# Cross-attention with image tokens: the values of the image tokens in four column tiles of TensorE, those of the last text tokens in two

## The chip, the core and the metric

The kernel runs on one core of a Trainium2 chip. The time is the device time of one execution in microseconds (us). TensorE (PE) multiplies and transposes into PSUM, VectorE (DVE), ScalarE (ACT) and GpSimd (POOL) work element by element, and all DMAs here are issued by SyncE (SP), whose queue is in order. Every engine runs its own instructions in order and waits for the others on semaphores.

## What is computed

Two batches of 2048 queries (640 wide) attend to 154 context tokens (1024 wide) in 20 heads of 32. The first 146 tokens are text; the last 8 are image tokens (4 dummies and 4 that carry a box mask), with key and value weights of their own and a softmax of their own. The two results are added, projected, and the input is added.

```python
text, ip_h = ctx[:, :146], ctx[:, 146:]
q = heads(x @ w_q)
out = merge(sdpa(q, heads(text @ w_k), heads(text @ w_v)))
out += merge(sdpa(q, heads(ip_h @ w_k_ip), heads(ip_h @ w_v_ip), mask=box_mask))
y = out @ w_out + b_out + x
```

## The kernel before

The queries are cut into 16 blocks of 256. A first iteration, the setup, makes the keys and values of both batches while it makes the queries and the maxima of scores of block 0. The 16 iterations behind it each finish one block and prepare the next. The instructions of every engine stand in an order written out by hand (`STEPS`), which all engines walk through; semaphores tie them together.

The change lies in the setup. The 154 tokens of a batch are split as 128 text tokens ("batch 0", "batch 1"), the last 18 text tokens ("rest", both batches together: 36 rows) and 8 image tokens ("ip", both batches: 16 rows). Their values are a product over 1024 = 8 chunks of 128 (`CC`), in plain fp32, 640 columns wide. `V_UNITS` (L93) lists eight units, two for each kind of token (512 and 128 columns); `V_PLACES` (L94) says ahead of which step a pair of units is made: ip ahead of the transposes X 0, rest ahead of the scores S(1,0), batch 0 ahead of S(2,0), batch 1 at the end of the setup. All of them are written by the matmul of L835, `make_values`.

What follows a unit:

- ACT copies it out of PSUM (L496 for ip and rest, L499 for batch 0 and 1) and counts `s_vc`.
- For batch 0 and 1, DVE splits the value in three bf16 parts: subtract from PSUM (L653, `v_left`), cast (L656, SBUF to SBUF), subtract again (L658, two inputs in SBUF). These stand in DVE's order ahead of the reductions of S(2,0) (L706, L707), which free the score banks for S(2,1) on PE.
- For ip and rest, SP moves 16 small pieces into `v_tail` (L362, L365), once `s_vc` says that both are copied.
- After batch 0, ACT converts the output weights (L528, `wo_hi`), and POOL makes their remainder (L438, `wo_lo`, one instruction on 128x3200).

Around this stand, in the setup: SP's 12 DMAs that build the key stack of batch 1 (L347, `k_stack`); POOL's two memsets of `k_tail` (L435), which wait for those DMAs to land, and stand ahead of `wo_lo` in POOL's order; on DVE the split of the maxima (L716 cast, L718), eight copies into `k_tail` (L666), and the split of batch 1. PE leaves the setup when the split of the last unit has read PSUM (`s_vsplit` at 10), among other waits, and begins iteration 1 with the transposes of L923.

Of the kernel before, what the change touches and what calls it, by code (L numbers as in the profile page):

```python
# [89 lines left out]

V_UNITS = [(keys, c0, c1) for keys in ("ip", "rest", "batch 0", "batch 1") for c0, c1 in ((0, 512), (512, D))]  # L93
V_PLACES = {("X", 0): (0, 1), ("S", 1, 0): (2, 3), ("S", 2, 0): (4, 5), None: (6, 7)}  # L94
W_O_PLACE = ("S", 2, 0)
COUNTS = {0: (0, 3), 1: (3, 4), 3: (4, 7), 4: (7, 8)}

# [66 lines left out]
def attention_kernel(nc, x, ctx, boxes, wq, wk, wv, wk_ip, wv_ip, wo, b_out,  # L164
# [5 lines left out]
    with ExitStack() as stack:  # L170
        def sb(name, shape, dt=F32, where=stack):
            return where.enter_context(nc.sbuf_tensor(name, shape, dt))
# [25 lines left out]
        with ExitStack() as setup:  # L198

            ctx_main = sb("ctx_main", [P, BATCHES, CTX_D], where=setup)  # L200
            ctx_rest = sb("ctx_rest", [P, CTX_D], where=setup)
            mask = sb("mask", [IP, SEQ], where=setup)

            w_k_ip = sb("w_k_ip", [P, CC, D], where=setup)

            w_kv = sb("w_kv", [P, CC, D], where=setup)
            ctx_t = sb("ctx_t", [P, CC, BATCHES * CTX], where=setup)
            rest_t = sb("rest_t", [P, CC, BATCHES * TAIL], where=setup)
            small = sb("small", [16, 256], where=setup)
            pick = sb("pick", [16, BATCHES * IP], BF16, setup)  # L210
            with ExitStack() as first:
                row_raw = sb("row_raw", [STACK - ROW_MASK, 4 * CTX], where=first)
                row_consts = sb("row_consts", [STACK - ROW_MASK, 4 * CTX], F32R, first)
            v_rest = sb("v_rest", [BATCHES * REM, D], where=setup)
            v_rest_ip = sb("v_rest_ip", [BATCHES * IP, D], where=setup)
            v_left = sb("v_left", [P, 512], where=setup)

        w_v_ip = wo_raw[:, 0:CC, :]
# [77 lines left out]
        def v_bank(n):  # L296

            return bank[4 + n % 4]
# [7 lines left out]
        def _(sp):  # L306
# [43 lines left out]
            def rest_of_setup():  # L350


                sp.wait_ge(s_vp, 2)
                sp.dma_start(wo_raw[:, KC:2 * KC, :], wo.rearrange("(c p) n -> p c n", p=P)).then_inc(s_wo, 16)
                keys_to_stack(1)

                sp.wait_ge(s_ones, 16 * BATCHES)
                sp.wait_ge(s_vc, 4)
                for b in range(BATCHES):
                    for j in range(4):  # L360
                        r = 32 * j
                        sp.dma_start(v_tail[b][r:r + REM, :, VW * j:VW * j + DH],  # L362
                                     v_rest[REM * b:REM * (b + 1), :].rearrange("p (g j d) -> p g j d", j=4, d=DH)[:, :, j, :]
                                     ).then_inc(s_vt, 16)
                        sp.dma_start(v_tail[b][r + REM:r + TAIL, :, VW * (4 + j):VW * (4 + j) + DH],  # L365
                                     v_rest_ip[IP * b:IP * (b + 1), :].rearrange("p (g j d) -> p g j d", j=4, d=DH)[:, :, j, :]
                                     ).then_inc(s_vt, 16)
# [97 lines left out]
        def _(act):  # L465
# [21 lines left out]
            def copy_values(units):  # L487

                for n in units:
                    keys, c0, c1 = V_UNITS[n]  # L490

                    act.wait_ge(s_vp, n + 1)
                    src = v_bank(n)[:, 0:c1 - c0]
                    if keys in ("ip", "rest"):
                        dst = v_rest_ip if keys == "ip" else v_rest
                        nc.scalar.activation(dst[:, c0:c1], src[0:dst.shape[0], :], ACT.Copy).then_inc(s_vc, 1)  # L496
                    else:
                        b = 0 if keys == "batch 0" else 1
                        nc.scalar.activation(v_main[b][:, c0 // DH:c1 // DH, 0:DH], src.rearrange("p (h d) -> p h d", d=DH),  # L499
                                             ACT.Copy).then_inc(s_vc, 1)  # L500
# [72 lines left out]
        def _(dve):  # L573
# [64 lines left out]
            def split_values(units):  # L638

                for n in units:  # L640
                    keys, c0, c1 = V_UNITS[n]
                    if keys in ("ip", "rest"):
                        continue

                    dve.wait_ge(s_vc, n + 1)
                    first, second, third = (v_main[0 if keys == "batch 0" else 1][:, c0 // DH:c1 // DH, c:c + DH]
                                            for c in (0, VW, VB))
                    left = v_left[:, 0:c1 - c0].rearrange("p (h d) -> p h d", d=DH)
                    done = V_PARTS * (n - 4)
                    if done:  # L650

                        dve.wait_ge(s_vsplit, done)
                    nc.vector.tensor_tensor(left, v_bank(n)[:, 0:c1 - c0].rearrange("p (h d) -> p h d", d=DH), first,  # L653
                                            ALU.subtract).then_inc(s_vsplit, 1)
                    dve.wait_ge(s_vsplit, done + 1)
                    nc.vector.tensor_copy(second, left).then_inc(s_vsplit, 1)  # L656
                    dve.wait_ge(s_vsplit, done + 2)
                    nc.vector.tensor_tensor(third, left, second, ALU.subtract).then_inc(s_vsplit, 1)  # L658
# [113 lines left out]
        def _(pe):  # L772
# [44 lines left out]
            def make_values(units):  # L817

                for n in units:
                    keys, c0, c1 = V_UNITS[n]  # L820
                    if n == 0:

                        pe.wait_ge(s_klo, 2 * GROUPS)
                        pe.wait_ge(s_mval, 2 * 4)
                        pe.wait_ge(s_wv_ip, 16)
                    if n == 2:
# [5 lines left out]
                    rows = {"ip": rest_t[:, :, BATCHES * REM:], "rest": rest_t[:, :, 0:BATCHES * REM],  # L832
                            "batch 0": ctx_t[:, :, 0:P], "batch 1": ctx_t[:, :, TEXT:TEXT + P]}[keys]
                    for c in range(CC):
                        last = nc.tensor.matmul(v_bank(n)[0:rows.shape[2], 0:c1 - c0], rows[:, c, :],  # L835
                                                (w_v_ip if keys == "ip" else w_kv)[:, c, c0:c1],
                                                start=(c == 0), stop=(c == CC - 1))
                    last.then_inc(s_vp, 1)

            def transpose_x(u, ps):  # L840
# [218 lines left out]
```

## Time and profile before

| | us |
|---|---|
| median of 3 runs | 805.45 (803.82 to 806.62) |
| span of the profiled execution | 801.8 |
| median less span | 3.65 |
| PE busy | 732.8 (91% of the span) |
| DVE busy | 565.4 (71%) |
| ACT busy, POOL busy | 287.3, 237.1 |
| mean granted TensorE clock | 0.981 of 2.4 GHz |
| setup: span's start to the first matmul of iteration 1 | 117.01 |
| eight units of values (L835), PE busy | 8.79 (ip), 9.73 (rest), 8.85, 8.85 |

The profile is of one execution, and no time beside its span is recorded for it, so its span is set against the median of the three runs. A matmul in fp32 appears as two records with a weight load each, so a unit of 8 matmuls shows 16. Starts and ends are in us from the span's start. "Idle before, released by" names what an engine waited for.

### The profile page before, as it was taken

The numbers are of one execution on the slowest core, as the hardware profiler recorded it, in microseconds if no ns is written. First come the engines' busy times: TensorE is split into PE (matmuls) and PEld (weight loads), VectorE is DVE, ScalarE is ACT, GpSimd is POOL, SyncE is SP. The second block draws the span as 40 slices with busy tenths as digits, with TensorE's granted clock in tenths as the row PEclk, the third lists the DMA queues.
The fourth block names the chain that finished last, engine by engine and source line by source line (L and its number), as shares of the span: only waits on it lengthen the run. The fifth ranks groups of instructions, "written<-read, shape, count | busy, mean of one in ns | idle before, by whom it ended". The sixth has DMA issues, their size and how long they took to land.

```text
span 801.8 us, 19010 instructions
## 1 busy us (share of the span) xinstructions
PE 732.8 (91%) x6384; PEld 645.1 (80%) x6384; DVE 565.4 (71%) x1694; ACT 287.3 (36%) x615; POOL 237.1 (30%) x347
## 2 busy tenths in 40 slices
PE   5968979999999999999999899999999999999887
PEld 4755458888888898989898888888898989898766
DVE  3241287778786968687878777786968686878774
ACT  1111026253443525151616152443525151616051
POOL 1000143324150606042423324150606051423334
PEclk9969999999999999999999999999999999999979
DMA  9989714344343525342424344343525342423220
GB/s 257 268 242 220 168 26 109 93 109 112 98 106 86 133 77 129 92 116 80 126 80 118 86 117 108 99 106 85 133 77 131 89 119 80 126 80 93 76 67 34
DMA packets 85115, 91.27 MB, mean 114 GB/s; under 512 B 10768, under 2 KB 69776, under 8 KB 85068
## 3 DMA queue, kind: packets, MB, share of 16 engines
q1 hardware_dynamic: 85084, 90.87, 43.6%
q8 instruction: 18, 0.29, 0.2%
q14 instruction: 13, 0.11, 0.0%
HBM read 40.42 MB, written 10.62 MB: 64 GB/s over the span
## 4 chain that ended last, share of the span: by engine, by line
PE 59%; DVE 18%; SPq 9%; issue 7%; DMA 7%; ACT 1%; DVEq 0%; ACTq 0%
PE psum L864 30%; PE psum L913 7%; PE psum L958 4%; SPq L407 4%; PE psum L939 4%; DVE p_lo L730 4%; PE psum L944 3%; DMA q_stack<-aux_a 3%; DVE o_parts L745 3%; DVE inv_den L737 2%; PE psum L835 2%; DMA q_stack<-mask_scratch 2%; DVE neg_max L706 2%; PE psum L982 2%; PE psum L799 2%
## 5 line engine op out<-in xcount | busy, mean ns | idle before, releaser
L450 POOL TENSOR_TENSOR attn<-o_parts 128x128 f32<-128x128 f32 x160 | 72.9, 456 | 443.0 <-DVE o_parts L742 443.0
L706 DVE TENSOR_REDUCE neg_max<-psum 128x2 f32<-128x292 f32 x320 | 144.1, 451 | 18.0 <-PE psum L913 14.8
L864 PE MATMUL psum<-wo_both,at_hi 128*128 128x320 f32 x640 | 154.1, 313 | 0.0
L730 DVE TENSOR_TENSOR p_lo<-p_whole,p_hi 128x512 f16<-128x512 f32 x160 | 137.1, 857 | 2.4 <-ACT p_hi L553 0.9
L913 PE MATMUL psum<-k_stack,q_stack 104*128 104x154 f32 x640 | 108.5, 284 | 20.0 <-DVE neg_max L707 13.4
L542 ACT ACTIVATE q_hi<-psum 128x256 fp32r<-128x256 f32 x80 | 30.7, 384 | 258.5 <-PE psum L864 258.5
L958 PE MATMUL psum<-v_tail,p_tail 128*128 128x264 f32 x320 | 105.5, 411 | 17.8 <-DVE p_lo L730 15.8
L864 PE MATMUL psum<-xt_hi,wq_hi 128*128 128x256 f32 x400 | 115.2, 288 | 1.0 <-DVE xt_lo L675 1.0
L913 PEld LDWEIGHTS psum<-k_stack,q_stack 104*128 104x128 f32 x640 | 89.6, 193 | 31.3 <-DVE neg_max L707 22.1
L864 PE MATMUL psum<-xt_lo,wq_hi 128*128 128x256 f32 x400 | 113.1, 283 | 0.0
L864 PE MATMUL psum<-xt_hi,wq_lo 128*128 128x256 f32 x400 | 113.0, 283 | 0.0
L552 ACT ACTIVATE p_whole<-psum 128x512 f32<-128x512 f32 x160 | 95.9, 599 | 44.2 <-PE psum L939 40.6
L864 PEld LDWEIGHTS psum<-wo_both,at_hi 128*128 128x128 f32 x640 | 109.7, 188 | 0.0
L455 POOL TENSOR_TENSOR attn<-attn,o_parts 128x128 f32<-128x128 f32 x160 | 104.8, 655 | 12.5
L864 PE MATMUL psum<-wo_both,at_lo 128*128 128x320 f32 x320 | 98.6, 308 | 0.0
L553 ACT ACTIVATE p_hi<-psum 128x512 f16<-128x512 f32 x160 | 95.6, 598 | 0.0
L697 DVE TENSOR_TENSOR q_lo<-psum,q_hi 128x256 fp32r<-128x256 f32 x80 | 34.0, 424 | 78.5 <-ACT q_hi L542 78.5
L763 DVE TENSOR_TENSOR out_sb<-psum,x_res 128x320 f32<-128x320 f32 x64 | 31.4, 491 | 66.4 <-PE psum L864 66.4
L864 PEld LDWEIGHTS psum<-xt_hi,wq_hi 128*128 128x128 f32 x400 | 77.2, 193 | 1.3 <-issue 1.3
L864 PEld LDWEIGHTS psum<-xt_hi,wq_lo 128*128 128x128 f32 x400 | 77.2, 193 | 0.0
L864 PEld LDWEIGHTS psum<-xt_lo,wq_hi 128*128 128x128 f32 x400 | 76.8, 192 | 0.0
L939 PE MATMUL psum<-q_stack,k_stack 120*128 120x256 f32 x320 | 69.8, 309 | 4.6 <-DMA q_stack<-aux_a 3.9
(87 smaller groups left out, 1331.4 us busy)
## 6 DMA issues: line engine op xcount, KB each, us to landing
q_stack<-q_hi SPq DMA_DIRECT2D x128, 96.0 KB
x_in<-in_x SPq DMA_DIRECT2D x16, 640.0 KB, 4.1
x_res<-in_x SPq DMA_DIRECT2D x16, 640.0 KB, 4.0
out<-out_sb SPq DMA_DIRECT2D x32, 320.0 KB
q_stack<-q_hi SPq DMA_DIRECT2D x128, 64.0 KB
q_stack<-q_lo SPq DMA_DIRECT2D x64, 96.0 KB
q_stack<-q_lo SPq DMA_DIRECT2D x64, 64.0 KB
q_stack<-aux_a SPq DMA_DIRECT2D x48, 64.0 KB, 2.3
```

Source lines behind the costliest of these rows:

```text
L407: sp.dma_start(q_stack[row:row + DH, 4 * g0 + j:4 * g1:4, :].bitcast(F32), src[DH * j:DH * (j + 1), g0:g1, :].bitcast(F32)).then_inc(stack ...
L450: nc.gpsimd.tensor_tensor(cols, o_parts[:, qt, 0:4, :], o_parts[:, qt, 4:8, :], ALU.add).then_inc(att_half, 1)
L455: nc.gpsimd.tensor_tensor(cols, cols, o_parts[:, qt, 8:12, :], ALU.add).then_inc(att_done, 1)
L552: nc.scalar.activation(p_whole[:, u, :, :].rearrange("p h q -> p (h q)"), src[:], ACT.Exp)
L553: nc.scalar.activation(p_hi[:, -g % P_SLOTS, 2 * u:2 * u + 2, :].rearrange("p h q -> p (h q)"), src[:], ACT.Exp).then_inc(exp_done, 1)
L697: nc.vector.tensor_tensor(q_lo[:, g, :], bank_a[:, 0:QB], q_hi[:, g, :].bitcast(F32), ALU.subtract).then_inc(gen_freed, 1)
L706: nc.vector.tensor_reduce(dst[:, :, 0], src[:, :, 0:TEXT], AX_X, ALU.max, negate=True)
L730: nc.vector.tensor_tensor(p_lo[:, -g % P_SLOTS, 2 * u:2 * u + 2, :], p_whole[:, u, :, :], p_hi[:, -g % P_SLOTS, 2 * u:2 * u + 2, :], ALU.s ...
L864: last = nc.tensor.matmul(ps, l(c), r(c), start=(i == 0), stop=(i == len(terms) - 1))
L913: last = nc.tensor.matmul(scores[(sc + pair) % 2][:, i * CTX:(i + 1) * CTX], q_stack[0:ROW_MAX, h, P * qt:P * (qt + 1)], k_stack[batch][0: ...
L939: last = nc.tensor.matmul(ps[:, QB * i:QB * (i + 1)], k_stack[batch][0:STACK, h, 0:P], q_stack[0:STACK, h, :], start=True, stop=True)
L958: nc.tensor.matmul(product_1[qt][:, 0:8, :], p_tail[:, -g % P_SLOTS, queries], v_tail[batch][:, g, :].rearrange("p (e d) -> p e d", d=VW), ...
```

## The change

The eight units become six: ip and rest are one unit each. For ip the 640 columns are regrouped as four sets of 160 (the heads 0, 4, 8, ..., then 1, 5, 9, ... and so on), and each set is multiplied by the same 16 stationary rows into a column tile of its own: PSUM partitions 32j to 32j+15. For rest there are two sets of 320 columns, into partitions 0 to 35 and 64 to 99. The chunks are the outer loop and the tiles the inner one, so neighbouring matmuls go to different tiles. ACT's copies become 4 (16x160) and 2 (36x320), the staging buffers `v_rest` and `v_rest_ip` get a partition range for each tile, and SP's DMAs into `v_tail` read from there: as many as before, of the same sizes. The counts of the waits follow the new number of units. The batches' units are as before, but lie in other banks.

```diff
-V_UNITS = [(keys, c0, c1) for keys in ("ip", "rest", "batch 0", "batch 1") for c0, c1 in ((0, 512), (512, D))]
-V_PLACES = {("X", 0): (0, 1), ("S", 1, 0): (2, 3), ("S", 2, 0): (4, 5), None: (6, 7)}
+V_UNITS = [("ip", 0, D), ("rest", 0, D)] + [(f"batch {b}", c0, c1) for b in range(BATCHES) for c0, c1 in ((0, 512), (512, D))]
+V_TEXT = 2
+V_PLACES = {("X", 0): (0,), ("S", 1, 0): (1,), ("S", 2, 0): (2, 3), None: (4, 5)}
...
-                sp.wait_ge(s_vp, 2)
+                sp.wait_ge(s_vp, 1)
...
-                sp.wait_ge(s_vc, 4)
+                sp.wait_ge(s_vc, V_TEXT)
...
+                    if keys == "ip":
+                        for j in range(4):
+                            rows = slice(32 * j, 32 * j + BATCHES * IP)
+                            last = nc.scalar.activation(v_rest_ip[rows, :, :].rearrange("p g d -> p (g d)"),
+                                                        v_bank(n)[rows, 0:GROUPS * DH], ACT.Copy)
+                        last.then_inc(s_vc, 1)
...
-                    for c in range(CC):
-                        last = nc.tensor.matmul(v_bank(n)[0:rows.shape[2], 0:c1 - c0], rows[:, c, :],
-                                                (w_v_ip if keys == "ip" else w_kv)[:, c, c0:c1],
-                                                start=(c == 0), stop=(c == CC - 1))
+                    if keys == "ip":
+                        heads = w_v_ip.rearrange("p c (g j d) -> p c g j d", j=4, d=DH)
+                        for c in range(CC):
+                            for j in range(4):
+                                last = nc.tensor.matmul(v_bank(n)[32 * j:32 * j + BATCHES * IP, 0:GROUPS * DH],
+                                                        rest_t[:, c, BATCHES * REM:], heads[:, c, :, j, :],
+                                                        start=(c == 0), stop=(c == CC - 1))
+                    elif keys == "rest":
+                        heads = w_kv[:].rearrange("p c (g j d) -> p c g j d", j=2, d=2 * DH)
+                        for c in range(CC):
+                            for half in range(2):
+                                last = nc.tensor.matmul(v_bank(n)[64 * half:64 * half + BATCHES * REM, 0:2 * GROUPS * DH],
+                                                        rest_t[:, c, 0:BATCHES * REM], heads[:, c, :, half, :],
+                                                        start=(c == 0), stop=(c == CC - 1))
```

PE's order around it, before (lines of the kernel before; `wo_raw` holds the value weights of the image tokens here, `w_kv` those of the text):

```order
L835 MATMUL psum<-wo_raw,rest_t 16x512 x8
L835 MATMUL psum<-wo_raw,rest_t 16x128 x8
L845 MATMUL psum<-ident,x_in 128x128 x4
L913 MATMUL psum<-k_stack,q_stack 128x154 x4
L845 MATMUL psum<-ident,x_in 128x128 x6
L913 MATMUL psum<-k_stack,q_stack 128x154 x4
L835 MATMUL psum<-w_kv,rest_t 36x512 x8
L835 MATMUL psum<-w_kv,rest_t 36x128 x8
L913 MATMUL psum<-k_stack,q_stack 128x154 x8
L835 MATMUL psum<-w_kv,ctx_t 128x512 x8
L835 MATMUL psum<-w_kv,ctx_t 128x128 x8
```

And the same place of PE in the changed kernel:

```order
L846 MATMUL psum<-wo_raw,rest_t 16x160 x32
L868 MATMUL psum<-ident,x_in 128x128 x4
L936 MATMUL psum<-k_stack,q_stack 128x154 x4
L868 MATMUL psum<-ident,x_in 128x128 x6
L936 MATMUL psum<-k_stack,q_stack 128x154 x4
L853 MATMUL psum<-w_kv,rest_t 36x320 x16
L936 MATMUL psum<-k_stack,q_stack 128x154 x8
L859 MATMUL psum<-w_kv,ctx_t 128x512 x8
L859 MATMUL psum<-w_kv,ctx_t 128x128 x8
```

No step has moved past another; 16 matmuls of ip became 32 narrower ones, 16 of rest became 16 of 320 columns. On ACT the place is this one, first before:

```order
L496 ACTIVATE v_rest<-psum 36x512
L496 ACTIVATE v_rest<-psum 36x128
L499 ACTIVATE v_main<-psum 128x16x32
L499 ACTIVATE v_main<-psum 128x4x32
L528 ACTIVATE wo_both<-wo_raw 128x3200
```

and now:

```order
L504 ACTIVATE v_rest<-psum 36x320 x2
L509 ACTIVATE v_main<-psum 128x16x32
L509 ACTIVATE v_main<-psum 128x4x32
L538 ACTIVATE wo_both<-wo_raw 128x3200
```

Here too only the two copies of rest differ; the conversion of the output weights (`wo_both`) still stands right behind the copies of batch 0. The orders of DVE and POOL are the same in both kernels.

## Rows read from the trace of the kernel before

**Rows 1.** The page, part 1: busy time, share, instructions
```profile
PE 732.8 (91%) x6384; PEld 645.1 (80%) x6384; DVE 565.4 (71%) x1694; ACT 287.3 (36%) x615; POOL 237.1 (30%) x347
```
**Rows 2.** Chain of waits, 30 to 150: start, us, what
```profile
74.91 5.20 DMA q_stack<-mask_scratch
...
82.66 9.66 PE psum L835 x32
...
106.71 6.36 DVE max_parts_a L716
...
116.33 0.30 DVE v_left L653
```
**Rows 3.** Timeline of PE, 66 to 118: start, us, engine, line, out<-in, count, idle before
```profile
67.05 8.79 PE L835 MATMUL psum<-wo_raw,rest_t 128*16 128x512 f32 x32
...
80.25 0.65 PE L913 MATMUL psum<-k_stack,q_stack 104*128 104x154 f32 x4 [3.82 <-DMA q_stack<-mask_scratch]
...
81.54 1.11 PE L913 MATMUL psum<-k_stack,q_stack 104*128 104x154 f32 x4
82.59 9.73 PE L835 MATMUL psum<-w_kv,rest_t 128*36 128x512 f32 x32
...
102.68 0.65 PE L913 MATMUL psum<-k_stack,q_stack 104*128 104x154 f32 x4
...
105.93 8.85 PE L835 MATMUL psum<-w_kv,ctx_t 128*128 128x512 f32 x32
117.01 0.42 PE L923 MATMUL psum<-ident,max_parts_a 128*80 128x128 f32 x2 [2.23 <-DVE v_main L656]
```
**Rows 4.** Timeline, 76 to 125: weight loads of rest, 12 steps apart
```profile
84.83 0.11 PEld L835 LDWEIGHTS psum<-w_kv,rest_t 128*36 128x36 f32 x1 [0.34 <-issue]
...
89.98 0.11 PEld L835 LDWEIGHTS psum<-w_kv,rest_t 128*36 128x36 f32 x1 [0.32 <-issue]
```
**Rows 5.** Windows: us, busy of PE, PEld, DVE, ACT, POOL, PEclk, DMA, GB/s
```profile
81.03:84.44 3.41, 3.41 (x12) 1.93 (x11) 2.59 (x10) 0.87 (x2) 0.00 (x0) 0.51 0.41 100
...
118.58:121.98 3.40, 3.40 (x19) 3.40 (x18) 1.17 (x6) 0.38 (x1) 0.00 (x0) 0.51 0.56 78
```
**Rows 6.** Timeline of ACT, 97 to 117.2
```profile
103.14 2.86 ACT L528 ACTIVATE wo_both<-wo_raw 128x3200 fp32r<-128x3200 f32 x1
```
**Rows 7.** Timeline of POOL, 97 to 117.2
```profile
98.02 4.40 POOL L435 MEMSET k_tail<- 128x2560 uint32 x2 [95.09 <-DMA k_stack<-k_tail]
106.08 6.93 POOL L438 TENSOR_TENSOR wo_both<-wo_raw,wo_both 128x3200 fp32r<-128x3200 f32 x1 [3.65 <-ACT wo_both L528]
```
**Rows 8.** Timeline of SP's queue, 84 to 107.2
```profile
85.24 9.01 SPq L347 DMA_DIRECT2D k_stack<-k_tail  x12
```
**Rows 9.** Timeline of DVE, 97 to 117.2
```profile
102.55 0.43 DVE L656 CAST v_main<-v_left 128x512 bf16<-128x512 f32 x1
103.01 0.69 DVE L658 TENSOR_TENSOR v_main<-v_left,v_main 128x512 bf16<-128x512 f32 x1
...
104.14 0.23 DVE L656 CAST v_main<-v_left 128x128 bf16<-128x128 f32 x1
104.40 0.29 DVE L658 TENSOR_TENSOR v_main<-v_left,v_main 128x128 bf16<-128x128 f32 x1
...
106.71 6.35 DVE L716 CAST max_parts_a<-neg_max 128x48 fp32r<-128x48 f32 x1
...
114.36 0.68 DVE L653 TENSOR_TENSOR v_left<-psum,v_main 128x512 f32<-128x512 f32 x1
```
**Rows 10.** Line L716: count, ns minimum, median, maximum, starts
```profile
L716 DVE CAST max_parts_a<-neg_max x16: 189/191/6351, 106.7 to 759.5; 128x48 fp32r<-128x48 f32 x16
```
**Rows 11.** Line L730, the same view
```profile
L730 DVE TENSOR_TENSOR p_lo<-p_whole,p_hi x160: 679/966/977, 126.7 to 784.2; 128x512 f16<-128x512 f32 x160
```
**Rows 12.** Timelines of POOL and DVE, 131.5 to 142
```profile
132.31 0.45 POOL L450 TENSOR_TENSOR attn<-o_parts 128x128 f32<-128x128 f32 x1 [19.31 <-DVE o_parts L742]
...
132.35 0.97 DVE L730 TENSOR_TENSOR p_lo<-p_whole,p_hi 128x512 f16<-128x512 f32 x1
```

More of the change, by code:

```diff
@@ L213, in attention_kernel @@
                 row_consts = sb("row_consts", [STACK - ROW_MASK, 4 * CTX], F32R, first)
-            v_rest = sb("v_rest", [BATCHES * REM, D], where=setup)
-            v_rest_ip = sb("v_rest_ip", [BATCHES * IP, D], where=setup)
+            v_rest = sb("v_rest", [P, GROUPS, 2, DH], where=setup)
+            v_rest_ip = sb("v_rest_ip", [P, GROUPS, DH], where=setup)
             v_left = sb("v_left", [P, 512], where=setup)
@@ L362, in rest_of_setup @@
                         sp.dma_start(v_tail[b][r:r + REM, :, VW * j:VW * j + DH],
-                                     v_rest[REM * b:REM * (b + 1), :].rearrange("p (g j d) -> p g j d", j=4, d=DH)[:, :, j, :]
+                                     v_rest[64 * (j // 2) + REM * b:64 * (j // 2) + REM * (b + 1), :, j % 2, :]
                                      ).then_inc(s_vt, 16)
                         sp.dma_start(v_tail[b][r + REM:r + TAIL, :, VW * (4 + j):VW * (4 + j) + DH],
-                                     v_rest_ip[IP * b:IP * (b + 1), :].rearrange("p (g j d) -> p g j d", j=4, d=DH)[:, :, j, :]
+                                     v_rest_ip[r + IP * b:r + IP * (b + 1), :, :]
                                      ).then_inc(s_vt, 16)
@@ L492, in copy_values @@
                     act.wait_ge(s_vp, n + 1)
[L493 to L496, printed above, removed]
+                    src = v_bank(n)[:, 0:c1 - c0] if n >= V_TEXT else None
+                    if keys == "ip":
[6 more added lines that the diff above has]
+                        for half in range(2):
+                            rows = slice(64 * half, 64 * half + BATCHES * REM)
+                            last = nc.scalar.activation(v_rest[rows, :, :, :].rearrange("p g j d -> p (g j d)"),
+                                                        v_bank(n)[rows, 0:2 * GROUPS * DH], ACT.Copy)
+                        last.then_inc(s_vc, 1)
                     else:
@@ L648, in split_values @@
                     left = v_left[:, 0:c1 - c0].rearrange("p (h d) -> p h d", d=DH)
-                    done = V_PARTS * (n - 4)
+                    done = V_PARTS * (n - V_TEXT)
                     if done:
@@ L825, in make_values @@
                         pe.wait_ge(s_wv_ip, 16)
-                    if n == 2:
+                    if n == 1:
                         pe.wait_ge(s_wv, 16 * GROUPS)
@@ L831, in make_values @@
                         pe.wait_ge(s_vc, n - 3)
-                    rows = {"ip": rest_t[:, :, BATCHES * REM:], "rest": rest_t[:, :, 0:BATCHES * REM],
-                            "batch 0": ctx_t[:, :, 0:P], "batch 1": ctx_t[:, :, TEXT:TEXT + P]}[keys]
-                    for c in range(CC):
-                        last = nc.tensor.matmul(v_bank(n)[0:rows.shape[2], 0:c1 - c0], rows[:, c, :],
-                                                (w_v_ip if keys == "ip" else w_kv)[:, c, c0:c1],
-                                                start=(c == 0), stop=(c == CC - 1))
+                    if keys == "ip":
[5 more added lines that the diff above has]
+                                                        start=(c == 0), stop=(c == CC - 1))
+                    elif keys == "rest":
+                        heads = w_kv[:].rearrange("p c (g j d) -> p c g j d", j=2, d=2 * DH)
+                        for c in range(CC):
+                            for half in range(2):
+                                last = nc.tensor.matmul(v_bank(n)[64 * half:64 * half + BATCHES * REM, 0:2 * GROUPS * DH],
+                                                        rest_t[:, c, 0:BATCHES * REM], heads[:, c, :, half, :],
+                                                        start=(c == 0), stop=(c == CC - 1))
+                    else:
+                        rows = {"batch 0": ctx_t[:, :, 0:P], "batch 1": ctx_t[:, :, TEXT:TEXT + P]}[keys]
+                        for c in range(CC):
+                            last = nc.tensor.matmul(v_bank(n)[:, 0:c1 - c0], rows[:, c, :], w_kv[:, c, c0:c1],
+                                                    start=(c == 0), stop=(c == CC - 1))
                     last.then_inc(s_vp, 1)
```

## The prediction

> **What bounds the kernel now.** I read the page first: PE is busy 732.8 of 801.8 us [rows 1], so PE time that is taken from the path counts one for one, and PE time taken beside a wait counts nothing. The change touches only the setup, the 117.01 us before iteration 1 [rows 3]; all later iterations are the same instructions and start when PE starts them, so the whole effect is how far that 117.01 moves, plus what the granted clock does around it.
>
> Second, the chain of waits through the setup [rows 2] together with PE's timeline [rows 3]. The reader is to see that the four units of values do not count alike. The ip units run from 67.05 to 75.84, and then PE waits 3.82 us for the mask rows of the query stack, which land at 80.11. That is the end of SP's line of issues, not of PE's work. The rest units, 82.59 to 92.32, are on the chain with 9.66 us. Behind them follow scores, batch 0, scores, batch 1, and then the chain is not PE's any more: it runs through a 6.36 us step of DVE (L716) and leaves by the last subtraction of the value split (L653), 0.4 us before 117.01.
>
> Third, DVE, POOL and ACT between 97 and 117 us [rows 6, 7, 9], to see why that step takes 6.36 us. It is a cast of 48 elements that takes 0.19 us in its other executions [rows 10]. Here it starts at 106.71 while POOL's `wo_lo` runs from 106.08 to 113.01, and it ends at 113.06. So it was held for the whole of POOL's instruction. The same is seen in the steady state: L730, a subtraction with both inputs in SBUF, takes 0.68 us alone and 0.97 us in the median [rows 11]; at 132.35 it starts while a POOL instruction runs until 132.76, and it ends 0.56 us after that [rows 12]. Both kinds of DVE instruction, the SBUF cast and the two-SBUF-input subtraction, stand still while a POOL tensor instruction runs. The value split of a unit has one of each (L656, L658).
>
> **The change, part by part.**
>
> *ip, PE.* 64 passes of 160 columns in place of 32. The weight loads of rest come 5.15 us apart over 12 steps [rows 4], which is the price of a pass: 0.429 us for 512 columns, or 0.134 for 160. One behind another that is 8.6 us, as now; with tiles side by side 4.3 or less. Either way it ends before 80.11, so it brings 0. ACT's four copies are short beside its 2.86 us for 3200 columns [rows 6] and fit in the same idle time.
>
> *A longer idle time ahead of 80.11, clock.* Now PE idles 3.8 us, and the granted clock fell to half (1.2 GHz) at 81.03, until 84.44 [rows 5]. With 8 us of idle I expect the half clock to be there already at 80.2. The four score matmuls then cost what the next four cost at half clock, 1.11 in place of 0.65 [rows 3], and the six transposes about as much more again: rest starts 0.9 later (0 to 1.1).
>
> *rest, PE.* 32 passes of 320 columns, 0.268 each. In a line: 8.6 us. Two at a time: 4.3, and 0.3 for the first pass, which has no partner, because a matmul's two passes are on the same tile and only its second can run beside the neighbour's first. No row of this trace has two column tiles, so both ends stand. I take side by side. The half clock adds about 0.3 (0 to 0.9; before, it cost some 0.9 of the 9.66). Sum: 9.66 - 4.9 - 0.9 = 3.9 us by which batch 0 begins earlier; 3.1 to 5.1 if the tiles run together, -0.8 if not.
> The Trainium skill, "TensorE: Matmul & The Clock Gate", Part 3, has three column tiles at 2.38 times the speed of one; by that the rest units would take about 5.4 us (estimate) and the shift would be 3.4. No run here shows it yet.
>
> *What the shift meets.* Three things do not move with PE. SP issues the 12 key-stack DMAs from 85.24 to 94.25 in its own line [rows 8]; POOL's memsets wait for their landing and stay at 98.02 to 102.42 [rows 7]; `wo_lo` comes behind them and behind ACT's conversion, which moves from an end at 106.00 to 102.1. So `wo_lo` starts at 102.4 to 102.9 in place of 106.08. In the kernel before, DVE's whole split of batch 0 (102.55 to 104.69 [rows 9]) fell into the gap between memsets and `wo_lo`. Moved by 3.9 it does not:
> - the first cast (L656) comes up at 98.65, inside the memsets. Does a memset hold a cast? No row shows the pair. Ends: no hold at all; held as L716 was by `wo_lo`, to the end of the instruction. The cast is one of the fast ones: it takes 0.43 us for 512 and 0.23 for 128 columns, half as much per column as the subtractions, 0.69 and 0.29 [rows 9], and L716 is another cast from SBUF to SBUF. I take the full hold.
> - held until the first memset ends (half of 4.40: 100.22), it pushes the second memset to about 102.75. The next casts come at 101.8 and wait for that; `wo_lo` is by then ready and waits as well. The small cast ends at 102.85, `wo_lo` takes over until 109.8, and the last subtraction (L658, two SBUF inputs) is shut out until then. It ends at 109.95 in place of 104.69: +5.3.
> - behind it in DVE's order stand the reductions of S(2,0), and PE waits for these with S(2,1), and behind that is batch 1. So batch 1 starts 5.3 late instead of 3.9 early, out of 11 us of idle: at half clock, +0.4 for the scores and about 1.3 for the units (3.4 us at half clock cost at most 1.7). Its last pass ends 7.0 later than now, at 121.8. DVE then splits: unit copied 120.65, subtraction, cast, subtraction 2.0 us as in rows 9, last subtraction done at 122.95, and 0.39 on to PE's start as now: 123.3, +6.3.
> - In exchange the idle time just before iteration 1 shrinks from 2.2 to 1.5 us, and the half clock of 118.58 to 121.98 [rows 5], worth at most 1.7, comes less often: -0.7 (0 to -1.7).
>
> Sum: +5.6, ends +4.1 (no half clock in either place) and +7.8 (the cast gets in only behind both memsets, +1, and the half clock stays). What the Trainium skill says in "SBUF — State Buffer", Who interferes with whom, is a rule against this change: DVE instructions in a 2-port mode and any GpSimd instruction shut each other out for the whole instruction, and one with two SBUF inputs is shut out only by a GpSimd instruction that reads SBUF. By that rule the cast is held by the memsets too, and the sum stands; the trace agrees on the two pairs that it has, and says nothing on the memset.
>
> *SP, DMAs.* The 16 pieces into `v_tail` stand behind the key-stack DMAs, which end at 94.25 [rows 8]; rest is copied by 89. No change.
>
> Against the median: 805.45 + 5.6 = 811.0.
>
> **The rivals.**
>
> *A, the memsets hold nothing.* Then the split of batch 0 runs at 97.9 to 100.8, batch 1 starts at 102.0, and `wo_lo` at 102.42, now bound by the memsets. L716 comes at 102.8 and is held until 109.4, the rest of the chain follows as now: the gain is 106.08 - 102.42 = 3.66, no more, whatever rest saves beyond it. 801.8. For it: no row has a hold by a memset. Against it: a cast was held by POOL once, for all of the time.
>
> *B, the tiles do not run together* (or the second pass of a tile blocks the queue). Rest takes 8.6 and the clock costs 0.9 more: 0.8 late. Split and `wo_lo` move together, as now. 806.0. For it: no row shows tiles at once.
>
> *C, a shift between 2.3 and 2.9.* `wo_lo` then waits for ACT (106.08 - 2.6 = 103.5) and the last subtraction slips in ahead of it. Batch 1 starts about 1.3 earlier and the end follows with some 1.9: 803.5. The last subtraction is due at 103.2 if the cast gets in between the memsets, so the forecast's mechanism decides where 106.08 less the shift is earlier than that: from 2.9 up (of 1.8 up if the cast has to wait for both memsets), and is at +5 at once: there is nothing in between.
>
> **How the numbers follow.** Forecast (shut out by `wo_lo`) 0.58, A 0.17, B 0.16, C 0.09. The forecast's own range is 809.5 to 813.3. For eight in ten the range must reach to A: 801.5 to 813.3. About 0.3% (2.4 us) is what can be told from no change. Faster by more: most of A and half of C, 0.20. Same: B, half of C, 0.20. Slower: the forecast and a little of B, 0.60.
>
> **What would show it.** Right: rest takes 4.6 to 5.5 us on PE and batch 0 starts near 90; a cast of L656's kind of 1.5 us or more inside the memsets; a subtraction of the 128-column unit that lasts about 7 us and ends just behind `wo_lo`; PE idle near 99 to 110; iteration 1 from 122 to 124. Wrong: rest near 8.6 (B), or short casts inside the memsets and a start of iteration 1 at 113.4 (A). The clock terms are wrong if PEclk is 1 at 80.3 or at 111. If ip ends after 80.1, the term of 0 is wrong as well.

## The result, and the profile after

The changed kernel is slower, as forecast: 811.04 us in the median of 20 runs (801.19 to 815.63), against 804.86 (802.83 to 807.89) in 20 runs of the kernel before on the same chip. The ratio is 1.0063 [1.0046, 1.008]; ratios here and below leave out runs that lie over 1.5% above the fastest of their kernel (here three, at 814.7 to 815.6, only because one ran at 801.19), so it lies a little below the quotient of the medians. The profiled execution took 808.35 us, of which 806.5 are its span: 4.7 more than the span of before. It is the lowest but one of the 20, and its mean granted clock, 0.975, is the highest of them (0.966 to 0.974 in the others), so the usual execution was a little slower than the one shown here.

The page, part 1:

```profile
PE 722.7 (90%) x6416; PEld 641.8 (80%) x6416; DVE 568.9 (71%) x1694; ACT 286.8 (36%) x617; POOL 237.3 (29%) x347
```

PE is busy 10.1 us less than in [rows 1] and the kernel takes longer: time went into waits. PE's timeline, 66 to 128:

```profile
66.59 2.37 PE L846 MATMUL psum<-wo_raw,rest_t 128*16 128x160 f32 x64
...
80.02 1.11 PE L936 MATMUL psum<-k_stack,q_stack 104*128 104x154 f32 x4 [10.48 <-DMA q_stack<-mask_scratch]
...
83.11 5.22 PE L853 MATMUL psum<-w_kv,rest_t 128*36 128x320 f32 x32
...
90.08 8.86 PE L859 MATMUL psum<-w_kv,ctx_t 128*128 128x512 f32 x32
...
110.09 1.16 PE L936 MATMUL psum<-k_stack,q_stack 104*128 104x154 f32 x4 [10.75 <-DVE neg_max L717]
111.05 10.98 PE L859 MATMUL psum<-w_kv,ctx_t 128*128 128x512 f32 x32
123.62 0.41 PE L946 MATMUL psum<-ident,max_parts_a 128*80 128x128 f32 x2 [1.59 <-issue]
```

Beside [rows 3]: ip takes 2.37 in place of 8.79 us, and the wait for the mask rows grows from 3.82 to 10.48; nothing is won there. Rest takes 5.22 in place of 9.73, and batch 0 begins 4.0 earlier. Then PE waits 10.75 us for DVE, and iteration 1 begins at 123.62, 6.61 later than before. What DVE did meanwhile is in its timeline, 97 to 112:

```profile
98.56 1.75 DVE L666 CAST v_main<-v_left 128x512 bf16<-128x512 f32 x1
100.35 0.69 DVE L668 TENSOR_TENSOR v_main<-v_left,v_main 128x512 bf16<-128x512 f32 x1
...
101.47 1.09 DVE L666 CAST v_main<-v_left 128x128 bf16<-128x128 f32 x1
102.59 6.99 DVE L668 TENSOR_TENSOR v_main<-v_left,v_main 128x128 bf16<-128x128 f32 x1
...
111.87 0.19 DVE L726 CAST max_parts_a<-neg_max 128x48 fp32r<-128x48 f32 x1
```

and in POOL's, over the same stretch:

```profile
97.80 4.68 POOL L436 MEMSET k_tail<- 128x2560 uint32 x2 [94.87 <-DMA k_stack<-k_tail]
102.53 6.91 POOL L439 TENSOR_TENSOR wo_both<-wo_raw,wo_both 128x3200 fp32r<-128x3200 f32 x1
```

The two read together: the split of batch 0, which took 0.43, 0.69, 0.23 and 0.29 us in [rows 9], now lies on POOL's instructions. The first cast comes 0.8 us into the first memset and stands still until that ends (half of the 4.40 of [rows 7], at 100.0); it gets in between the two, and both memsets together take 4.68. The second cast stands until the second memset ends at 102.48. The last subtraction comes up at 102.59, 0.06 us behind the start of `wo_lo`, and ends at 109.58, 0.14 behind its end. The maxima's cast, which had this place in [rows 9], takes 0.19. The subtraction of 100.35 ran beside the second memset and was not held: 0.69 us. That is the rule of the Trainium skill, "SBUF — State Buffer", Who interferes with whom, by which a DVE instruction with two SBUF inputs is shut out only by a GpSimd instruction that reads SBUF; a memset only writes. The trace agrees.

The chain of waits, 60 to 128, has the held instruction where [rows 2] had the maxima's cast:

```profile
83.18 5.15 PE psum L853 x32
...
102.59 6.99 DVE v_main L668
110.09 1.16 PE psum L936 x4
111.26 10.79 PE psum L859 x32
123.62 0.41 PE psum L946 x2
```

And the granted clock, in windows (us, busy of PE, PEld, DVE, ACT, POOL, then PEclk, DMA share, GB/s):

```profile
80.02:84.50 4.48, 4.48 (x20) 3.53 (x22) 2.85 (x10) 0.87 (x2) 0.00 (x0) 0.50 0.38 89
85.00:101.50 16.50, 13.93 (x70) 7.60 (x66) 5.45 (x13) 4.00 (x5) 3.70 (x2) 1.00 0.78 177
102.00:110.00 8.00, 0.00 (x0) 0.00 (x0) 7.97 (x5) 0.01 (x1) 7.39 (x2) 0.50 0.05 7
110.09:115.00 4.91, 4.91 (x9) 2.73 (x10) 2.93 (x16) 0.00 (x0) 0.00 (x0) 0.50 0.00 0
123.62:130.00 6.38, 6.14 (x50) 5.73 (x50) 3.93 (x15) 1.38 (x4) 0.00 (x0) 1.00 0.56 118
```

The half clock (1.2 GHz) is there from the first score matmul at 80.02, it meets the first 5 us of work behind the long idle time, and it is absent at the start of iteration 1, where the kernel before had it [rows 5].

### The profile page after: what moved, and what is told of

It is laid out like the page before. It is cut to its first block, busy times and chain, and to the rows that moved or that the text cites. A ratio compares the mean times of both kernels' runs of the same rounds, so it can differ in the third digit from the quotient of the medians.

```text
span 806.5 us, 19076 instructions
## 1 busy us (share of the span) xinstructions
PE 722.7 (90%) x6416; PEld 641.8 (80%) x6416; DVE 568.9 (71%) x1694; ACT 286.8 (36%) x617; POOL 237.3 (29%) x347
## 4 chain that ended last, share of the span: by engine, by line
PE 58%; DVE 16%; SPq 10%; DMA 8%; issue 7%; ACT 1%; DVEq 0%; ACTq 0%
PE psum L887 28%; PE psum L936 7%; SPq L408 5%; PE psum L981 4%; PE psum L962 4%; DMA q_stack<-aux_a 3%; PE psum L967 3%; DVE p_lo L740 3%; DVE o_parts L755 3%; DMA q_stack<-mask_scratch 2%; PE psum L859 2%; DVE inv_den L747 2%; PE psum L809 2%; PE psum L1005 2%; SPq L381 2%
## 5 line engine op out<-in xcount | busy, mean ns | idle before, releaser
L716 DVE TENSOR_REDUCE neg_max<-psum 128x2 f32<-128x292 f32 x320 | 144.5, 453 | 20.8 <-PE psum L936 17.8
```

Of the source, the lines that this page charges most:

```text
L716: nc.vector.tensor_reduce(dst[:, :, 0], src[:, :, 0:TEXT], AX_X, ALU.max, negate=True)
```

## The experiments

Theory T: the tiles bring the split of batch 0 into the memsets and against `wo_lo`; DVE's SBUF cast and its subtraction of two SBUF inputs stand still for as long as such an instruction runs; the granted clock takes a part of what is left. Rivals: the loss is in the tiles themselves (ip, or PE's order), or in the clock alone, or the lock is incidental. Each kernel was timed in five rounds beside the kernel before on the same chip; the median of before was 802.9 beside experiments 1 to 5 and 8 to 10, and 803.36 beside 6, 7, 11 and 12. Experiments 2, 3, 5 and 11 are the kernel before with a part changed, the others the changed kernel; of the longer edits only the main lines are shown.

**1. `wo_lo` waits for the split** (e1), on POOL ahead of `wo_lo`:

```diff
+            pool.wait_ge(s_vsplit, 2 * V_PARTS)
```

> The changed kernel, with one wait more: GpSimd begins the remainder of the output weights (wo_lo) only when VectorE has split both units of batch 0. Theory 'shut out' (the last subtraction of the split stands still while wo_lo runs, and with it the reductions that PE waits for): that subtraction takes 0.29 us again, wo_lo starts near 102.9 in place of 102.53, batch 1 starts near 104.2 in place of 111.05, iteration 1 near 114.4 in place of 123.6; about 802.5 us, 8 faster than the changed kernel and 2.5 faster than the kernel before. Rival 'clock' (the loss comes from the long idle time and the half clock behind it, not from the lock): wo_lo 0.4 us later changes nothing, 811.

Measured 803.29 us, ratio 1.0006 [0.9991, 1.002], span 800.2. Timeline, 100 to 118, of DVE, POOL and PE:

```profile
102.15 0.29 DVE L669 TENSOR_TENSOR v_main<-v_left,v_main 128x128 bf16<-128x128 f32 x1
102.59 6.94 POOL L440 TENSOR_TENSOR wo_both<-wo_raw,wo_both 128x3200 fp32r<-128x3200 f32 x1 [0.55 <-DVE v_main L669]
103.91 11.32 PE L860 MATMUL psum<-w_kv,ctx_t 128*128 128x512 f32 x32
116.78 0.41 PE L947 MATMUL psum<-ident,max_parts_a 128*80 128x128 f32 x2 [1.56 <-issue]
```

`wo_lo` begins only 0.06 us later than in the changed kernel, and the subtraction takes 0.29 in place of 6.99: who comes first decides 6.84 us at the start of iteration 1. In this execution the subtraction, at 102.15, might have come first even without the wait, as ACT's conversion ended only at 102.20; what the wait does is seen in the runs: none of the twelve is above 806.41, where 19 of the first 20 of the changed kernel, and seven of twelve in experiment 6, are above 808. The whole loss is gone. But the start was to be at 114.4 and is at 116.78: batch 1 took 11.32 us in place of 8.85, at half clock (window of e1):

```profile
102.00:108.50 6.50, 5.55 (x10) 2.97 (x11) 6.08 (x11) 0.20 (x1) 5.95 (x2) 0.50 0.06 9
```

**2. The lock without any tile** (e2), the kernel before with ACT's conversion, and so `wo_lo`, one step ahead:

```diff
-W_O_PLACE = ("S", 2, 0)
+W_O_PLACE = ("S", 1, 0)
```

> The kernel before, without any column tile; only ScalarE's conversion of the output weights stands ahead of batch 0 in its order, so that wo_lo can start right behind the memsets of k_tail, near 102.5 in place of 106.08. Theory 'shut out': the split of batch 0 starts at 101.8, its first cast waits for the memsets and meets wo_lo; one DVE instruction of the split lasts about 7 us, batch 1 starts near 111 to 113, iteration 1 near 122 to 124: 809 to 812 us. Rival 'the tiles themselves cost' (their layout, copies or DMAs): no tiles, so no loss; wo_lo ends 3.6 earlier, the maxima's cast is free earlier, 803 to 805.

Measured 809.54 us, ratio 1.0092 [1.0078, 1.0106]. Timelines of DVE and POOL:

```profile
103.21 7.30 DVE L658 TENSOR_TENSOR v_main<-v_left,v_main 128x512 bf16<-128x512 f32 x1
102.77 7.20 POOL L438 TENSOR_TENSOR wo_both<-wo_raw,wo_both 128x3200 fp32r<-128x3200 f32 x1
```

The split lies within 0.2 us of where it lay in before; only ACT's conversion and with it `wo_lo` came earlier, and iteration 1 begins at 124.70. The tiles are not needed for the loss.

**3. Only ip in tiles** (e3: the kernel before with the ip unit of the change, rest as it was).

```diff
-V_UNITS = [(keys, c0, c1) for keys in ("ip", "rest", "batch 0", "batch 1") for c0, c1 in ((0, 512), (512, D))]
+V_UNITS = [("ip", 0, D), ("rest", 0, 512), ("rest", 512, D)] + [...]
...
```

> Only the image tokens in four column tiles, the last text tokens as before. Theory: ip lies beside SP's issues, so its 6.4 us less bring nothing; the longer idle time puts the half clock at 80.2 and makes rest start 0.5 later. Rest ends near 92.8, no trap: 805.5, within 1 us of before. Rival 'the PE time counts': 6 us faster.

Measured 803.53, ratio 1.0019 [1.0005, 1.0033]; ip takes 2.37 us, PE then waits 10.59, and iteration 1 begins at 116.58. ip brings nothing; by the ratio it costs 0.4 to 2.6 us, and no experiment says where. The score matmuls began 0.7 earlier than in before (79.52 against 80.25) and rest at the same time (82.61), so the half clock on them costs those 0.7. That it is the longer idle time that brings it is not shown: in experiment 2, with ip as before, PE waited 3.68 us and the same matmuls ran at half clock too (1.11 us from 79.51), where the kernel before waited 3.82 and had them at full clock.

**4. The same tiles, one after another** (e4): the tile is the outer loop, the chunk the inner one.

```diff
-                        for c in range(CC):
-                            for j in range(4):
+                        for j in range(4):
+                            for c in range(CC):
...
```

> The changed kernel with the tile as the outer loop and the 8 chunks as the inner one, so that a tile's matmuls follow each other and no neighbour is in another tile. Theory: without neighbours in other tiles nothing runs together: rest takes 8.6 us plus the half clock, some 9.5; ip 8.6; batch 0 starts 0.5 to 1 later than in the kernel before, no trap: 805 to 806.5. Rival 'fewer columns of the array are what is fast': rest 5.2 as in the changed kernel, and the trap, 811.

Measured 803.93, ratio 1.0013 [0.9996, 1.003]. Timelines of PE and of its weight loads:

```profile
66.66 7.29 PE L846 MATMUL psum<-wo_raw,rest_t 128*16 128x160 f32 x64
82.86 8.81 PE L853 MATMUL psum<-w_kv,rest_t 128*36 128x320 f32 x32
...
87.17 0.69 PEld L853 LDWEIGHTS psum<-w_kv,rest_t 128*36 128x36 f32 x7 [0.16 <-issue]
```

Same instructions, same tiles, and little gain: 8.81 us for rest against 5.22 in the changed kernel, 7.29 for ip against 2.37. Within a tile the weight loads of rest come 0.27 us apart, one for each pass; only at the change of tile, at 87.17, come seven in 0.69 us. So tiles run together where neighbours in the order go to different ones, and the little that is gained lies at the changes of tile. That is rival B made real; its time, about the old one, is what the prediction gave it.

**5. Only rest in tiles** (e5: the kernel before with the rest unit of the change).

```diff
-V_UNITS = [(keys, c0, c1) for keys in ("ip", "rest", "batch 0", "batch 1") for c0, c1 in ((0, 512), (512, D))]
+V_UNITS = [("ip", 0, 512), ("ip", 512, D), ("rest", 0, D)] + [...]
...
```

> Only the last text tokens in two column tiles, the image tokens in one, as before. Theory 'shut out': rest alone makes the shift of about 3.6 us that lets the split of batch 0 meet the memsets and wo_lo, so the loss of the changed kernel is all here: one subtraction of about 7 us, iteration 1 near 123, 5 to 6 us above the kernel before. Rival 'both parts share the loss': 2 to 4 us above it.

Measured 806.77, but in two groups: 797.5 to 798.4 (four of twelve) and 804.6 to 810.05 (eight); ratio 1.0022 [0.9987, 1.0058], a mean over the two, without the upper four of the second, that says little. The profiled execution is one of 797.5. Timelines of DVE and POOL, 96 to 103:

```profile
96.80 0.43 DVE L662 CAST v_main<-v_left 128x512 bf16<-128x512 f32 x1
98.39 1.36 DVE L662 CAST v_main<-v_left 128x128 bf16<-128x128 f32 x1
99.78 0.29 DVE L664 TENSOR_TENSOR v_main<-v_left,v_main 128x128 bf16<-128x128 f32 x1
97.44 4.48 POOL L436 MEMSET k_tail<- 128x2560 uint32 x2 [94.50 <-DMA k_stack<-k_tail]
101.97 6.93 POOL L439 TENSOR_TENSOR wo_both<-wo_raw,wo_both 128x3200 fp32r<-128x3200 f32 x1
```

Here the mask rows had landed early (the scores began at 78.55, against 80.02 in the changed kernel), the first cast was over 0.2 us before the memsets began, only the small one was held, and the split was done 1.9 us ahead of `wo_lo`. Iteration 1 began at 113.18. The start of the scores lies between 78.55 and 80.76 in the profiled executions of all kernels, and a shift of that size between DVE and POOL would decide between a gain of 5 us on the 802.9 of before and a loss of 2 to 7. That the executions from 804.6 to 810.05 were held is inferred; none of them was profiled.

**6. The changed kernel again** (a2), without an edit:

> The changed kernel once more, beside the three others on this chip, for its distance to them and for how its single times are spread: 5 to 8 us above the kernel before in most executions, a few near 801 (the first cast is through before the memsets begin, or the last subtraction ahead of wo_lo) and a few near 815 (the first cast waits for both memsets).

Measured 809.49 in the median: 801.49 to 804.55 in five of twelve runs and 809.0 to 813.65 in seven, where the first twenty runs had only one below 808; ratio 1.0028 [0.9998, 1.0058]. The profiled execution, 811.2, lost the race in another way. Timelines of DVE and POOL:

```profile
99.18 3.44 DVE L666 CAST v_main<-v_left 128x512 bf16<-128x512 f32 x1
103.77 6.43 DVE L666 CAST v_main<-v_left 128x128 bf16<-128x128 f32 x1
97.93 4.40 POOL L436 MEMSET k_tail<- 128x2560 uint32 x2 [95.00 <-DMA k_stack<-k_tail]
102.71 7.41 POOL L439 TENSOR_TENSOR wo_both<-wo_raw,wo_both 128x3200 fp32r<-128x3200 f32 x1 [0.37 <-ACT wo_both L538]
```

The first cast came 1.25 us into the memsets and waited for both, and the small cast met `wo_lo`. Iteration 1 at 124.35. This is the case that the prediction put at its upper end (the cast behind both memsets, the half clock stays): the span is 7.6 above before's, +7.8 was given.

**7. `wo_lo` in five pieces** (e6):

```diff
-            nc.gpsimd.tensor_tensor(wo_lo, wo_raw[:, KC:2 * KC, :], wo_hi.bitcast(F32), ALU.subtract).then_inc(s_wsplit, 1)
+            for k in range(KC):
+                last = nc.gpsimd.tensor_tensor(wo_lo[:, k, :], wo_raw[:, KC + k, :], wo_hi[:, k, :].bitcast(F32), ALU.subtract)
+            last.then_inc(s_wsplit, 1)
```

> The changed kernel with wo_lo in five instructions of 128x640 (some 1.4 us each) in place of one, and nothing else. Theory 'shut out': an instruction of VectorE that comes up waits for the piece that runs, not for the whole; the subtraction of the 128-column unit takes at most 1.5 us and batch 1 starts near 105 in place of 111: 4 to 6 us below the changed kernel. Rival 'GpSimd keeps the lock from one instruction to the next': the subtraction still takes 7 us, no difference.

Measured 802.66, ratio 0.9983 [0.9966, 1.0], 6.8 below the changed kernel on the same chip. Timelines of DVE and POOL:

```profile
102.15 1.61 DVE L670 TENSOR_TENSOR v_main<-v_left,v_main 128x128 bf16<-128x128 f32 x1
102.08 7.54 POOL L440 TENSOR_TENSOR wo_both<-wo_raw,wo_both 128x640 fp32r<-128x640 f32 x5
```

The subtraction waits for one piece in place of all: the lock is held for an instruction, not for as long as POOL has work.

**8. Idle time filled** (e9): experiment 1, and four matmuls of 512 columns behind S(2,0) on PE; their results are overwritten later.

```diff
+                            for c in range(FILL):
+                                nc.tensor.matmul(v_bank(0)[:, 0:512], ctx_t[:, c, 0:P], w_kv[:, c, 0:512], start=True, stop=True)
...
```

> The changed kernel with wo_lo waiting for the split of batch 0, and four matmuls of 512 columns more on PE behind the scores of S(2,0), into a bank that nobody reads before it is overwritten. They fill PE's idle 3.4 us (99.5 to 102.95) and compute nothing that is used. Theory 'clock': the granted clock stays at 1 through batch 1, which takes 8.9 in place of 11.3 us, and iteration 1 begins near 114.4 in place of 116.8: 2 us below the kernel with the wait alone, and below the kernel before, unless the fall of the clock then comes behind iteration 1's start. Rival 'batch 1 was slow for another reason' (GpSimd or VectorE beside it): still 11.3 us, 803.

Measured 800.14, ratio 0.9967 [0.9954, 0.998]: 3.1 below experiment 1 (each beside 802.9 of before), for work that nobody needs. Batch 1 ran at full clock although it began 1.4 later:

```profile
105.27 8.86 PE L861 MATMUL psum<-w_kv,ctx_t 128*128 128x512 f32 x32
```

Iteration 1 begins at 115.69, 1.09 earlier than in experiment 1. The profiled execution is one of the slowest of its twelve (802.27), with a span no shorter than experiment 1's (800.5 against 800.2), so its trace shows what batch 1 gained, and not where the rest of the 3.1 lies.

**9. The split behind the maxima** (e7): experiment 1, and DVE's split of batch 0 moved behind the reductions of S(2,0) and S(2,1) and the maxima's cast.

```diff
-                        split_values(V_PLACES.get((kind, *args), ()))
...
+                    split_values(V_PLACES[("S", 2, 0)])
...
```

> The changed kernel with wo_lo waiting for the split of batch 0, and VectorE's order changed: the reductions of S(2,0) and S(2,1) stand ahead of the split of batch 0, which comes after the maxima's cast. PE then waits for no split ahead of batch 1. Theory: S(2,1) runs at about 99.8, batch 1 from 100.5 at the full clock to 109.3; the end of the setup is then VectorE's, behind wo_lo (104 to 111): iteration 1 near 115, 2 us below the kernel before. Rival 'iteration 1 hangs on something else' (the pieces of v_tail, SP): no better than the kernel with the one wait, 803.

Measured 803.37, ratio 1.0 [0.9987, 1.0014]: no gain. PE no longer waits for the split, batch 1 begins at 101.16 and takes 8.85, but the next casts in DVE's order meet `wo_lo`:

```profile
105.06 7.97 DVE L677 CAST k_tail<-k_stack 120x130 fp32r<-120x130 f32 x8
```

They take 1.22 otherwise. PE is idle 5.58 us again, and iteration 1, begun at 115.59 as expected, runs at half clock until 120.1. Whatever stands there in DVE's order pays.

**10. `wo_lo` on DVE** (e8): no POOL tensor instruction in the setup, ACT's conversion one step ahead, the order of experiment 9.

```diff
-            nc.gpsimd.tensor_tensor(wo_lo, wo_raw[:, KC:2 * KC, :], wo_hi.bitcast(F32), ALU.subtract).then_inc(s_wsplit, 1)
...
+                        nc.vector.tensor_tensor(wo_lo, wo_raw[:, KC:2 * KC, :], wo_hi.bitcast(F32), ALU.subtract
+                                                ).then_inc(s_wsplit, 1)
...
```

> As the kernel with the maxima first, but no GpSimd tensor instruction in the setup at all: ScalarE converts the output weights ahead of batch 0, and VectorE makes the remainder (3.5 us) ahead of the reductions of S(2,0). Theory: wo_lo at 97.5 to 101, batch 1 from 102 to 111, casts held by the memsets only until 102.4, split of batch 1 at once: iteration 1 near 113, 4 us below the kernel before. Rival: VectorE's 3.5 us more on the path cancel it: no difference from the kernel with the maxima first.

Measured 796.3 (794.1 to 797.95), ratio 0.9908 [0.9889, 0.9928]: faster than both kernels. Timelines of DVE and PE:

```profile
93.87 3.49 DVE L699 TENSOR_TENSOR wo_both<-wo_raw,wo_both 128x3200 fp32r<-128x3200 f32 x1 [2.86 <-ACT wo_both L536]
100.68 8.85 PE L861 MATMUL psum<-w_kv,ctx_t 128*128 128x512 f32 x32
111.10 0.41 PE L948 MATMUL psum<-ident,max_parts_a 128*80 128x128 f32 x2 [1.56 <-issue]
```

DVE takes half of POOL's time for it, in an idle stretch, and no DVE instruction is held any more.

**11. The same without tiles** (e10: the kernel before, with the edit of experiment 10).

> The kernel before, without tiles, but with the order of the kernel that has wo_lo on VectorE: output weights converted ahead of batch 0, wo_lo on VectorE, the reductions of S(2,0) and S(2,1) ahead of the split of batch 0. It tells what the tiles bring once nothing can be shut out. Theory: S(2,1) no longer waits for the split (1.9 us less), batch 1 from 104.4 to 113.3, iteration 1 near 115, 2 us below the kernel before; the kernel with the tiles has it at 111.1, so the tiles are worth 3 to 4 us there. Rival 'the new order is all of the gain': as good as with the tiles, 6 to 7 us below before.

Measured 799.26, ratio 0.9931 [0.9913, 0.995]; iteration 1 at 114.85. So the tiles are worth 3.75 us at that start once nothing is locked, and some 2 in the ratio (0.9931 less 0.9908, times 803), whose intervals overlap. Most of the gain comes without the tiles, from `wo_lo` on DVE and the new order together; the two were not tried apart.

**12. The first idle time filled too** (e11): experiment 10 with ten matmuls of 512 columns, results overwritten, in PE's wait for the mask rows.

```diff
+                            for c in range(FILL):
+                                nc.tensor.matmul(v_bank(1)[:, 0:512], ctx_t[:, c % CC, 0:P], w_kv[:, c % CC, 0:512],
+                                                 start=True, stop=True)
...
```

> The kernel with wo_lo on VectorE, and ten matmuls of 512 columns more on PE in its idle time of 9.7 us behind the transposes X 0 (some 70 to 79), whose results are overwritten. Theory 'clock': PE does not fall to the half clock at 79.6 to 85.3; the scores, the transposes and rest cost some 2 us less, iteration 1 near 109, 2 us below the kernel with wo_lo on VectorE. Rival: the half clock is there hidden behind DMAs or VectorE, no difference.

Measured 796.8, ratio 0.9909 [0.9889, 0.9929]: missed, no gain. Rest ran at full clock (4.50 us) and batch 0 began 3.5 earlier than in experiment 10, at 86.72; 1.0 of that is that the mask rows landed earlier (scores from 78.58, against 79.59). Then S(2,1) waited for DVE, which was at `wo_lo`, the clock fell behind that wait, and the maxima's cast met the second memset:

```profile
99.52 2.24 DVE L728 CAST max_parts_a<-neg_max 128x48 fp32r<-128x48 f32 x1
```

Iteration 1 at 110.89, against 111.10. The same pattern as the change itself: work that comes earlier meets what did not move.

## Why the prediction was right

Sign, mechanism and place were right, and the size of the change nearly so: +5.6 forecast, +6.2 between the medians. By its steps:

| step | forecast | trace |
|---|---|---|
| ip in tiles | brings 0 | brings 0 (experiment 3) |
| half clock already at 80.2; rest starts later by | 0.9 | 0.5 (83.11); 0.75 counted from the first score matmul |
| rest, on the path | 4.9 | 5.15 |
| batch 0 begins earlier by | 3.9 | 3.99 |
| first cast held until | 100.22 | 100.31 |
| small cast ends | 102.85 | 102.56 |
| last subtraction ends | 109.95 | 109.58 |
| batch 1, more than at full clock | 1.3 | 2.13 |
| iteration 1 begins | 123.3 (+6.3) | 123.62 (+6.61) |
| given back behind it | 0.7 | 1.9: 0.9 by the start of iteration 2, 1.0 in the last 41 us |
| sum, on the span | +5.6 | +4.7 |

The terms that were mis-sized are both the clock's. Batch 1 was given 3.4 us at half clock, the length of the stretches in [rows 5]; here it lasted from 110.09 to 115.3, and in experiment 1 from the start of the scores at 102.95 to 108.8. And the give-back was put at 0.7 and came to 1.9, in two places. PE's first matmul of iteration 2 and the windows from the start of iteration 16 to the end of the span show them, in each pair first before, then changed:

```profile
L923 PE MATMUL psum<-ident,max_parts_a x2: 270/270/271, 161.4 to 161.5; 128*80 128x128 f32 x2
L946 PE MATMUL psum<-ident,max_parts_a x2: 270/270/271, 167.1 to 167.2; 128*80 128x128 f32 x2
...
760.90:801.80 40.90, 32.39 (x272) 27.86 (x269) 25.23 (x69) 13.99 (x29) 14.27 (x21) 0.87 0.17 49
766.60:806.50 39.90, 31.10 (x271) 26.82 (x269) 25.06 (x69) 13.75 (x29) 14.25 (x21) 0.91 0.17 51
```

From iteration 1 to iteration 2 it is 44.4 us before and 43.5 now: 0.9 is given back there, close to the 0.7 forecast. The starts of iteration 16 are 5.7 apart, as those of iteration 2 are. The other 1.0 lies in the last 41 us, where a second stretch at half clock took some 10.6 us before and 7.2 now (estimates from the mean clocks 0.87 and 0.91). That place is not in the prediction, which held that behind iteration 1 nothing but the clock around its start would differ; why the clock fell for a shorter time there is open. What bears out the first part: where the half clock met the start of iteration 1 (before, experiments 3, 4, 6, 9, 10), iteration 2 begins 44.4 to 45.6 us behind it; where it did not (the changed kernel and experiments 1, 2, 5, 7, 8, 11, 12), 42.7 to 43.7. For the whole rest of the span the two sets overlap, 684.5 to 686.0 and 680.9 to 684.8 us.

The ends of the sum do not follow from the terms named for them. Without batch 1's half clock (0.4 and 1.3) and with the give-back in full (1.7) the sum is +2.9, where +4.1 is stated; with the cast 1.0 later and no give-back it is +7.3, where +7.8 is. Experiment 6, which has that case, lies at +7.6: 7.3 at the start of iteration 1 and 0.3 behind it.

That 811.0 meets the median of 811.04 so closely is luck. The forecast stood on 805.45, the median of three runs before; the twenty beside the result have 804.86. That start was 0.6 too high, and the change of +5.6 was 0.6 too small. The median also comes from a mixture of runs. The two profiled executions of the changed kernel, 4.7 and 7.6 above before's span, stand for two ways of losing the same race, and the median lies between; the runs at 801 to 804.6 (one of the first 20, five of the 12 of experiment 6) seem to have won it. The prediction had the two ways of losing (its ends), but took the outcome as one per kernel and did not say that it would be drawn anew in each run.

Wrong without an effect on the time: the reasoning that only a matmul's second pass can run beside its neighbour's first. By it the 64 passes of ip would take 4.3 us; they took 2.37, 0.037 each against 0.134 for 160 columns alone, 3.6 at a time. Rest at full clock steps 0.27 us for two passes, exactly two at a time. The Trainium skill, "TensorE: Matmul & The Clock Gate", Part 3, has 2.38 for three tiles; these runs show 2.0 for two and 3.6 for four.

The rivals: A (memsets hold nothing) falls with the casts of 1.75, 1.09 and 3.44 us. B falls with rest's 5.22, and experiment 4 shows what it would have been. C needs a shift below 2.9; it was 3.99.

Where the saved time went once the split is not held: experiment 1 was to begin iteration 1 at 114.4 in place of 117.01 and to be 2.5 faster than before. It was no faster. Batch 1's half clock took 2.5 us of it (11.32 against 8.85), and experiment 8 shows the cause: with the wait filled, batch 1 took 8.86 and the median fell by 3.1.

Open: what decides at the boundary of the two memsets. Casts that came 0.4 to 1.4 us after POOL's record began (the changed kernel, experiments 1, 5 and 7) got in between; those that came 1.25 and 1.9 us after it (experiments 6 and 8) did not. So it is not the order of arrival alone. How often each side of the race comes up in the changed kernel is not known either (one of 20 and five of 12 near 801 to 804.6), nor was a run near 801 profiled.

## What to carry to other kernels

When PE's work gets shorter, write down which DVE instructions move and lay them on GpSimd's timeline: an SBUF-to-SBUF cast, or a subtraction with both inputs in SBUF, that comes up 0.06 us after a GpSimd instruction of 7 us has begun costs 7 us. Order such pairs by a wait, cut the long instruction in pieces, or take it off GpSimd. And price an idle time of TensorE twice: the wait, and the half clock that may meet the work behind it.

## What the runs showed of the hardware

- A wait of PE's that ended 3.4 us after it began (experiment 1) made the next units 2.5 us longer; eight passes of unneeded work in it (3.64 us, experiment 8) made them run at full clock. The last wait alone does not tell: behind one of 1.86 us batch 1 took 8.85 in experiment 3 and 10.55 in experiment 4.
- The lock works both ways. `wo_lo` takes 6.9 us alone, and 7.41 where a subtraction of two SBUF inputs had begun 0.06 us ahead of it (experiment 6), 7.20 where a cast had (experiment 2). DVE makes the same 128x3200 subtraction in 3.49 us.
- The same program on one core took 797.5 to 798.4 us in some executions and 804.6 to 810.05 in others (experiment 5). A race between DVE's and POOL's instructions fits, as the traces of other kernels show both sides of it; no execution near 809 of that kernel was profiled.
